# An attention and expert kernel on one core: the last rounds' order on VectorE, an early function table, and products while rows are awaited

## The reference

```python
x = x + attention(layernorm(x), ctx, ctx, w_q, b_q, w_k, b_k, w_v, b_v, w_o, b_o)
h = layernorm(x)
probs = softmax(h @ router_w)            # 8 experts
top_w, top_i = top_k(probs, 2)
for e in range(8):
    y = silu(h @ gate_w[e]) * (h @ up_w[e])
    out = out + cw[:, e:e + 1] * (y @ down_w[e])   # cw: top_w at the chosen experts, 0 elsewhere
x = x + out
```

## Time and profile before

| | us |
|---|---|
| three runs | 1023.01, 1024.22, 1024.89 (median 1024.22) |
| the profiled execution | 1023.31 |
| its span, first to last instruction | 1021.5 |
| TensorE busy | 895.0 (88%) |
| VectorE busy | 624.3 (61%) |
| ScalarE busy | 477.6 (47%) |
| GpSimd busy | 245.7 (24%) |
| mean granted TensorE clock | 0.928 |

### The profile page before, as it was taken

One profiled execution on the slowest core, in us unless ns is written; L12 is line 12 of the kernel. 1 busy time (PEld: TensorE's weight loads), 2 busy tenths in 40 slices (PEclk: granted clock), 3 DMA queues, 4 the chain that ended last, 5 costly groups with the idle time before them and its releaser, 6 DMA issues.

```text
span 1021.5 us, 32114 instructions
## 1 busy us (share of the span) xinstructions
PE 895.0 (88%) x12208; PEld 795.2 (78%) x12208; DVE 624.3 (61%) x1943; ACT 477.6 (47%) x903; POOL 245.7 (24%) x299
## 2 busy tenths in 40 slices
PE   1689888888888886269999999999999999999996
PEld 1467666666666665168999999989999999999995
DVE  5778777777677775445745744744654756644443
ACT  2668666666666665133533522522432434432321
POOL 2102333333333322511211211211211212221111
PEclk9889888888888887579999999999999999999999
DMA  6011221222222241126252432252252252222221
GB/s 215 20 39 46 68 60 61 59 68 75 69 64 58 58 169 43 66 69 176 33 155 54 106 85 57 35 155 36 49 155 53 33 155 54 32 31 36 36 34 16
DMA packets 69072, 73.57 MB, mean 72 GB/s; under 512 B 19724, under 2 KB 62810, under 8 KB 69018
## 3 DMA queue, kind: packets, MB, share of 16 engines
q1 hardware_dynamic: 44986, 32.98, 11.4%
q0 software_dynamic: 12944, 17.87, 10.2%
q10 hardware_dynamic: 11088, 22.02, 6.1%
HBM read 45.18 MB, written 26.39 MB: 70 GB/s over the span
## 4 chain that ended last, share of the span: by engine, by line
PE 48%; issue 5%; DMA 4%; DVE 3%; ACT 3%; POOL 1%; another core or an unknown queue 1%; ACTq 0%; SPq 0%; POOLq 0%; DVEq 0%
PE bank L472 11%; PE bank L474 10%; PE bank L473 10%; PE bank L662 5%; PE bank L663 5%; PE bank L664 5%; DMA raw<-expert_rows 4%; PE bank L637 1%; PE bank L526 1%; POOL expert_rows L1317 1%; DVE h_full L1198 1%; ACT pt_hi L728 1%; ACT h_hi L802 1%; ACT g_act L800 1%
## 5 line engine op out<-in xcount | busy, mean ns | idle before, releaser
L472 PE MATMUL bank<-xg,e_hi 128*128 128x128 f16 x2176 | 373.0, 220 | 0.7 <-DVE xg L1175 0.6
L473 PE MATMUL bank<-xg,e_hi 128*128 128x128 f16 x2176 | 373.0, 220 | 0.0
L474 PE MATMUL bank<-xg,e_lo 128*128 128x128 f16 x2176 | 373.0, 220 | 0.0
L1344 POOL DMA_INDIRECT out<-y_sb,tok_row x68 | 113.5, 1670 | 466.5 <-DVE y_sb L1193 442.9
L472 PEld LDWEIGHTS bank<-xg,e_hi 128*128 128x128 f16 x2176 | 213.2, 98 | 2.0 <-issue 0.8
L473 PEld LDWEIGHTS bank<-xg,e_hi 128*128 128x128 f16 x2176 | 213.2, 98 | 0.7
L474 PEld LDWEIGHTS bank<-xg,e_lo 128*128 128x128 f16 x2176 | 213.2, 98 | 0.0
L800 ACT ACTIVATE g_act<-bank 128x512 f32<-128x512 f32 x136 | 81.2, 597 | 249.3 <-PE bank L474 234.0
L1198 DVE SCALAR_TENSOR_TENSOR h_full<-bank,g_act 128x512 f32<-128x512 f32 x136 | 94.1, 692 | 129.9 <-ACT g_act L800 122.3
L662 PE MATMUL bank<-e_hi,h_hi 128*128 128x256 f16 x544 | 148.4, 273 | 3.9 <-DVE h_lo L1204 3.9
L663 PE MATMUL bank<-e_lo,h_hi 128*128 128x256 f16 x544 | 148.3, 273 | 0.0
(11 more groups left out here) (172 smaller groups left out, 1809.6 us busy)
## 6 DMA issues: line engine op xcount, KB each, us to landing
raw<-expert_rows SPq DMA_DIRECT2D x68, 132.5 KB, 2.6
e_stage<-in_gate_w ACTq DMA_DIRECT2D x7, 1024.0 KB
e_stage<-in_up_w ACTq DMA_DIRECT2D x7, 1024.0 KB
e_stage<-in_down_w ACTq DMA_DIRECT2D x7, 1024.0 KB
expert_rows<-pads SPq DMA_DIRECT2D x8, 530.0 KB
xin<-in_x SPq DMA_DIRECT2D x16, 256.0 KB, 2.9
xres<-in_x SPq DMA_DIRECT2D x16, 256.0 KB
out<-x SPq DMA_DIRECT2D x16, 256.0 KB
```

The costliest lines, as they stand in the source:

```text
L472: pe.matmul(dst, a_hi(c), b_hi(c), start=c == 0, stop=False)
L473: pe.matmul(dst, a_hi(c), b_lo(c), start=False, stop=False)
L474: mm = pe.matmul(dst, a_lo(c), b_hi(c), start=False, stop=ends and c == chunks - 1)
L1344: pool.indirect_dma_start(out, bass.IndirectOffsetOnAxis(tok_row[:], 0), y_sb[:], None, compute_op=ALU.add).then_inc(added, 16)
```

## The change

Three edits.

- VectorE: the last three rounds (batch `z` there, `b` and `n` empty, `z` of the epilogue) leave the general body and run `draining`: weights of `z` to their end, `normalize(c, 1)`, slots of `z` to their end, `high_rows(r)`, then `low_att`, `residual`, `sum_x`, and the steps of `statistics` and `route_top` in turns. In the same rounds ScalarE puts the second norm for `r` at unit 0.
- ScalarE: after the last round one Silu of a single element into `silu_seed`, ahead of the wait for `tables_ready`.
- TensorE: after the last round, 24 products of a constant f16 identity with 512 columns of `w_hi` into `banks[0]`, ahead of the wait for `tables_ready`. The wait for `shifted` before them is for the last reader of that bank.

```diff
+FILLERS = 24
...
+        silu_seed = sb("silu_seed", [1, 1])
...
+            pe.wait_ge(shifted, B * UNITS)
+            for _ in range(FILLERS):
+                pe.matmul(banks[0][:], ident16[:], w_hi[:, 0, :, :].rearrange("p c d -> p (c d)"), start=True, stop=True)
             pe.wait_ge(tables_ready, 3)
...
-                extra = {0: [(a, lambda j: norm(j, 0, xin, xn, xt_turned, 1, xn_ready, m))],
+                extra = {0: [(a, lambda j: norm(j, 0, xin, xn, xt_turned, 1, xn_ready, m)),
+                             (not b and r, lambda _: norm(r, 1, x2, x2n, row_ready, 2, x2n_ready, m))],
                          1: [(a, split_x), (c, split_att)],
-                         2: [(r, lambda j: norm(j, 1, x2, x2n, row_ready, 2, x2n_ready, m))],
+                         2: [(b and r, lambda _: norm(r, 1, x2, x2n, row_ready, 2, x2n_ready, m))],
...
+            act.activation(silu_seed[:], ident[0:1, 0:1], ACT.Silu).then_inc(seeded, 1)
             act.wait_ge(tables_ready, 3)
...
+                if not b and z and z.reg is None and not n:
+                    draining(c, r, z)
+                    return
...
+            def draining(c, r, z):
+
+                def run(chain):
+                    for _ in chain:
+                        pass
+
+                if c:
+                    low_probs(c, UNITS - 1)
+                run(combine_weights(z, z.plus % 2))
+                if c:
+                    normalize(c, 1)
+                run(take_slots(z, z.plus % 2))
+                if r:
+                    high_rows(r, r.plus % 2)
+                top_chain = route_top(r) if r else ()
+                if c:
+                    low_att(c)
+                    residual(c)
+                    sum_x(c, 1, x2, x2_ready, 1, x2_summed)
+                    for _ in statistics(c + 3, None, c):
+                        next(top_chain, None)
+                run(top_chain)
```

More of the change, by code:

```diff
@@ L217, in build @@
         passed = sem("passed")
+        seeded = sem("seeded")
         w_in = sem("w_in")
```

## The result

| | before | after |
|---|---|---|
| median of 9 runs each, us | 1022.27 (1021.03 to 1024.89) | 1018.59 (1017.26 to 1020.45) |
| ratio, 95% interval | | 0.9961 [0.9951, 0.9970] |
| profiled execution, us | 1023.31 | 1017.75 |
| median in a second comparison, us | 1023.10 | 1019.44, ratio 0.9969 [0.9958, 0.9979] |

The changed kernel is faster by 3.7 us in both comparisons, 0.3 to 0.4%. The forecast was 1019.7 in a range of 1016.7 to 1021.8, built from a gain of 4.55 us. So the time is in the range, and the gain is 0.9 us smaller than its sum.

The account below looks back on a forecast made before the run. Between attention and expert stages a chain of small steps through all engines was the bound, no busy engine. Order 3.3 plus table 1.25 gave 4.55 us, constant products nothing: 1019.7 against the median 1024.22, range 1016.7 to 1021.8.

Parts of the forecast that it names:

- The order: VectorE's last three rounds, with ScalarE's early norm: slots and indirect DMAs come earlier, first rows at TensorE 3.3 us sooner.
- The added wait: VectorE, third-last round: thirteen statistics steps queue behind TensorE's logits for batch 14; last step at 418.05, still 1.3 us earlier.
- The norm on ScalarE: ScalarE's two norms for batch 14, about 1.1 us, move ahead of `split_att` into idle time; nothing there gets late.
- The table: ScalarE's table load moves from before the first Silu to behind the last `router_exp`: 1.25 us gained, bounds 0 and 1.30.
- The constant products: 24 TensorE products before the first expert rows: cost nothing, taken as no gain; bounds 1.8 us gained, 1.7 lost.
- The look-ahead of 18 products: TensorE's sequencer passes the constant products with 18 left, at about 428.4, so count reads end at 435.4 before the rows.
- The warm start: Rival, chance 0.18: the clock outlives the hole and the expert stage starts at 2.4 GHz, 1.8 us less, 1017.0.
- bound of 1.7 lost: Constant products' lower bound: a late clock fall makes the half clock cover 3.4 us more of the dense expert start.
- Part of the gain lost to `low_att` beside GpSimd's subtraction: Rival, 0.12 together with a repeated table load: the order gives only 2.0 us, time about 1021.0.
- The table loaded again: Rival, sharing the 0.12 of a partial loss: ScalarE loads the table again at L800, time about 1021.0.
- Reads behind the fillers: Rival, 0.05: TensorE's count reads wait for an empty array, ending 2.6 to 4.4 us after the rows; 1022.3 to 1024.1.
- Slower: Rival, 0.03: constant products at half clock throughout, count reads end 5.9 us after the rows; 1026.4.

Follow-up runs that it names:

- The experiment with six steps ahead: Products among the reads, plus six statistics steps on VectorE before it waits for batch 14's logits, where the change does one: 1017.64, ratio 0.9952.
- the best order: Changed kernel's order and table with six statistics steps before the logits of batch 14: 0.9952 with 34 constant products, 0.9958 (1018.14) with none.
- the kernel with the norm back at unit 2: Changed kernel with ScalarE's second norm for `r` put back behind `split_att`; VectorE's order stays: 1021.41 against 1022.77, ratio 0.9985.
- products among the reads: Changed kernel with 10 constant products ahead and 3 behind each of TensorE's eight count reads, 34 in all, instead of 24: 1018.25, ratio 0.9961.
- rows before zero rows: Products among the reads with six statistics steps first; SyncE also reads each second tile's rows before writing the next expert's zero rows: 1016.94, ratio 0.9948.

## Why the prediction was right, and where its sum was not

**The order: 3.3 forecast, 3.2 measured.** The table in the first section holds the step by step: from the slots of 13 to the first indirect DMA of 15 no step is off by more than 0.3 us, apart from the landing of 13, which is 0.5 earlier (2.51 for the 2.84 of the earlier trace rows) and on which nothing waits any more. In the four profiles without the order the first indirect DMA of 15 comes at 26.16, 25.86, 25.93 and 25.92, mean 25.97; in the four with all of it (after twice, order alone, order with table) at 22.96, 22.97, 22.53 and 22.51, mean 22.74. The first rows at TensorE go from a mean of 34.69 to one of 31.46. Both are 3.2.

**The added wait** was called by its mechanism and costs what the prediction's steps gave it. It had taken the last statistics step at 12.79; it came at 13.03. The experiment with six steps ahead shows the price of that choice, 1.0 us, inside the bounds of the order.

**The norm on ScalarE** was said to be needed in half a sentence ("nothing on it gets late"). The run without it shows it as the larger half of the order's gain: 2.0 us of 3.2 at the indirect DMAs, 2.3 us in the medians. The prediction argued only that the move does no harm; it should have priced it.

**The table: 1.25 forecast, 1.0 measured; the term was over-sized.** From the rows to the first result tile, profiles without products take 15.73, 15.83 and 16.06 us with the old table load (mean 15.87) and 14.85, 15.00 and 14.81 with the early one (mean 14.89). The wait of 1.24 at the first down product is gone in whole, as forecast. But more of the first 48 products ran at the half clock in these (38, 41 and 37, against 30, 32 and 37 with the late load), at 0.05 us more each: 5.7 more on the mean, 0.28 us, which is the missing quarter. Whether that goes with the edit or is chance, three profiles of each don't settle. The medians have 1.2 by itself (0.9986) and almost nothing on top of the order (961.18 and 960.90); 1.0 lies within both intervals.

On the disputed price the rows are plain. The load takes 1.28 us and the seed starts 1.30 after it, in after as in the earlier trace rows; moving it brought 1.0. The Trainium skill ("ScalarE: Activation LUTs", What ACT_TABLE_LOAD costs) adds a drain of about 1.38 us, which would have made it 2.66. No run here shows that drain; in all of them ScalarE is idle ahead of the load or has just ended one small instruction.

**The constant products: 0 forecast; nothing that the medians can tell, and 0.6 to 0.9 at the start in the profiles.** Two pairs of medians: 1.0011 [0.9992, 1.0031] alone, and 0.9952 against 0.9958 on top of the best order. The products end at 28.56, within the 27.4 to 29.2 of the forecast, and the reads end at 29.91 (forecast 30.1), 1.4 ahead of the rows. The look-ahead of 18 products, taken from two rows, held with 36; with 24 it was not put to the test, since the counts themselves were ready only when 17 or 18 products were left. The warm start was given 0.18, and a clock that falls in the hole was the base case. What came is between them: in after the clock was still full when the rows came and fell at 436.2, as the stretch table shows (TensorE busy, other engines, clock, DMA share, GB/s):

```profile
429.00:430.00 1.00, 1.00 (x5) 0.39 (x4) 0.00 (x0) 0.00 (x0) 0.79 (x1) 0.81 1.00 348
...
436.00:437.00 1.00, 1.00 (x16) 1.00 (x13) 0.00 (x0) 0.00 (x0) 0.00 (x0) 0.60 0.89 278
...
439.00:440.00 1.00, 1.00 (x16) 1.00 (x14) 0.00 (x0) 0.00 (x0) 0.00 (x0) 0.69 0.00 0
```

Then 32 of the first 48 products ran at the half clock (26 in the second profile of after), as many as in before (30 and 32), but fewer than in the three profiles with the early table and no products (41, 38 and 37): against these the products do bring something. The two profiles of after are 0.6 and 0.9 us below the 14.89 from rows to first result tile. That is what the products back at the full clock (7 and 13 fewer, at 0.05 us each) and the transposes (0.40 for 0.61) add up to, 0.5 and 0.8. All six profiles with the early table, constant products and a hole of at most 3.7 us lie below all three without products: 13.44 to 14.32 against 14.81 to 15.00. Where the hole was over 4 us nothing came: the products alone (4.26) are 0.4 above the 15.87 without them, and the kernel with the norm back at unit 2 (4.15) has 15.07. The medians, with intervals of more than 1 us, neither show this nor exclude it. The prediction's bound of 1.7 lost, for a late fall, had this mechanism; its size did not come.

**The rivals.** Part of the gain lost to `low_att` beside GpSimd's subtraction: fallen. `low_att` took 0.69 us at 405.88, while the subtraction ran from 405.40 to 406.52. The table loaded again: fallen, no load at L807. Reads behind the fillers: fallen at 24; at 36 the reads are late, though not by waiting for an empty array as this rival had it. There the ratio goes from 0.9969 to 0.9977 (0.7 us in the medians; the intervals overlap, the trace decides it) and the transposes come 2.1 to 2.9 us later. Slower: nothing of it.

**What was off: the anchor, and the gain that reached the medians.** The prediction set 4.55 against the median of three runs, 1024.22. Nine runs of before in the same comparison have 1022.27, and 1022.27-4.55=1017.7 would have been 0.9 too low; 1024.22-4.55=1019.7 came out 1.1 too high. Two errors of opposite sign: the anchor 1.95 too high, the gain 0.9 too large. That the number itself came out so near owes something to luck. Nor does lying in the range say much by itself, as its upper end, 1021.8, is only 0.5 below what before takes; the steps in the profiles are the better evidence for the mechanism. The reason given for the anchor, that a later rise of the clock would put other runs above the profiled one, isn't borne out: seven of the nine runs of before lie below the 1023.31 of the profiled one. And in the second profile of before, which took 1023.69, the rise came only 2 products later (32 of the first 48 at the half clock, for 30), 0.1 us; it was 0.7 earlier at the first result tile and lost its time behind it.

**Where the 0.9 went.** Up to the first result tile the two pairs of profiles gain 5.24 and 4.06 us, mean 4.65, against 4.55 forecast: up to here the sum holds, though not term by term (the table brought less than forecast, the products more). From there to the last tile before takes 557.19 and 558.88, after 558.87 and 559.33. These four differ almost only in TensorE's wait for rows at the changes of expert. Its waits from 455 to 1015 (total us, times, longest), in after:

```profile
PE bank L640 <- DMA raw<-expert_rows: 7.0, 6, 1.4
```

and, in the same view of the two profiles of before:

```profile
PE bank L637 <- DMA raw<-expert_rows: 5.7, 6, 1.5
```

```profile
PE bank L637 <- DMA raw<-expert_rows: 7.3, 6, 1.4
```

The kernel before has 5.7 in one execution and 7.3 in another, so this much is chance from execution to execution. Over all fourteen profiles first to last tile takes 557.2 to 559.3 us, and TensorE's idle time for raw rows in that stretch 5.7 to 7.8. Take the one from the other, and 551.4 to 551.8 are left in every profile, with and without the change. So this one wait is nearly the whole of the spread, and 1.4 of the 1.7 us that the first pair lost. The four without the new order have a mean of 557.8 from first to last tile (6.3 of it the wait), the ten with it one of 558.2 (6.6), and one of before is among the four longest. The spread of 2 us is twice the missing 0.9. So the profiles place the missing part behind the first result tile, mostly in that wait, where the change puts nothing, but the difference of the means, 0.4, is too small beside the spread to be called a cost of the change. It isn't excluded either. What makes the rows late by more or less at a change of expert was not looked for, and stays open.

## What to carry to other kernels

Where a pipeline drains, a general loop body orders its work for a full pipeline: in the last rounds list what each next transfer waits for, put those steps first on every engine that touches them (here VectorE's order without ScalarE's lost half of the gain), and place each remaining step by when its input comes, not by which chain it belongs to. Size such a gain by laying profiles on each other at the last event before the changed part, since two executions of one kernel differ by more than a microsecond in parts that were not touched. Work that only keeps the clock up must end close to the real work and yet not hold the reads on its own queue; here it shortened the start by 0.6 to 1.4 us where the hole left was under 4 us, by nothing where it was longer, and the medians can't tell either from no change.

## What the runs showed of the hardware

**On one chip the kernel is nearly 6% faster.** The kernel before takes 964.67 us on one chip (962.56 to 969.50 in 24 runs) and 1022 to 1024 on the others. All of it lies in attention: the last `normalize` comes at 347.5 on that one and at 405.3 and 404.8 on the others; the time from there to the last tile differs by under 2 us. The pages' clock rows, of the order alone on the fast chip and of the second profile of before on another:

```profile
PEclk9989999999999965999999999999999999999999
```

```profile
PEclk9989888888888888589999999999999999999999
```

After the first few rounds the one chip holds its clock in every slice of attention, the other falls a tenth short in every slice: from 50 us on to 50 us before the last `normalize` the mean granted clock is 0.99 on the one and 0.87 in the profiles of before. The instructions of that stretch are the same and in the same order, so what starts it isn't in the program; whether the clock is the whole of it was not looked for, and its cause stays open. The change brought 3.8 us there (order and table) and 3.7 here.

**The clock outlives an idle hole of a few microseconds, but not safely.** In after it was still full 1.5 us behind a hole of 2.76, and fell. With 4.26 us of hole it fell within it (the products alone). With a hole of 1.71 us it stayed up in one profile (products among the reads), and in two other kernels with the same products and holes of 1.38 (with the six steps) and 1.51 (rows before zero rows) it fell 1.6 and 1.7 us after work resumed. The Trainium skill ("TensorE: Matmul & The Clock Gate", Part 1) has idle gaps bring the half rate back. These rows agree, with the addition that the fall can come after work has resumed.
